# Keeping the output projection's weights in SBUF, and moving the sum of the keys

## The chip, the cores and the metric

The kernel runs on one core of one Trainium2 chip. The metric is the device time of one execution in microseconds (us); a number of executions is given as its median. All arithmetic is in float32.

## The reference

One decoder layer in three parts, each added to its input and followed by a layer norm. `x` is 4 sequences of 1024 tokens of width 512.

```python
# part 1: Mamba block with gated MLP
xz = rmsnorm(x) @ in_proj_w.T;  u, z = split(xz)          # 1024 channels each
u = silu(causal_conv(u, 4 taps) + conv_b)
dt_r, B, C = split(u @ x_proj_w.T);  dt = softplus(dt_r @ dt_proj_w.T + b)
h_t = exp(dt * A) * h_(t-1) + dt * B * u                  # 16 states per channel, over 1024 tokens
y = (sum over states of h * C + u * D) * silu(z)
h = x + y @ out_proj_w.T                                  # the output projection, 1024 -> 512
x = layernorm(x + h + (silu(n @ w1.T) * (n @ w2.T)) @ w3.T),  n = rmsnorm(h)
# part 2: cross attention on 64 keys, 16 heads; a temperature per head and sequence
scores = q @ k.T / sqrt(32)
feats = [mean of scores, mean of the row maxima, mean variance of softmax(scores)]
t = exp(clip(mlp(feats)));  attn = softmax(q @ k.T / (2 t))
x = layernorm(x + (attn @ v) @ Wo.T + bo)
# part 3: linear layer plus a mixture of 8 rank-16 experts, top 2
x = layernorm(x + x @ W.T + b + lora(x))
```

## The kernel before

The 4096 tokens are cut into 8 chunks of 512 (two to a sequence), and the work of each chunk into small units, each a few instructions on one or several engines. There are five streams of units, and every engine runs the units of all streams in one fixed order:

- the scan ("step", "sum", "gate"): 64 steps to a chunk, each for 2 blocks of 128 channels and one state. POOL (GpSimd) multiplies by B (L1194) and by C (L1204), ScalarE (ACT) makes the decays with an exponential (L1252), DVE (VectorE) runs the recurrence (L1558) and adds up the states (L1568). After 16 steps the gate (L1574) multiplies the finished pair of blocks by silu(z). Four gates make a chunk's y;
- the "f" stream: first the fronts of all 8 chunks (norm, transposes, "cv" and "z" blocks of the input projection with the convolution, the small projection "proj"), and only then, chunk by chunk, the output projection. Unit `("ou", c, half, q)` is piece q of 4 of its weights for half of chunk c's tokens: 4 matmuls at L1839. "out" adds x and squares (DVE L1585, ACT L1337), "rms" and "hs" make the norm (ACT L1344), "to" transposes (L1849);
- the "y" stream: the gated MLP ("h", "hv" at L1781, "w3" at L1878), its layer norm, "turn" (transposes, L1891) and the query projection (L1781);
- the "s" stream: scores for the statistics. For each of a chunk's 4 tiles of 128 tokens and each half of the heads: "sc1" (TensorE, L1914), "mx" (DVE maximum, L1640), "e1" (ACT exponentials, L1428), "sq" (DVE sum, L1653). "ent" closes the chunk. At every second chunk "mean" (L1668 to L1676) gathers the sequence's statistics into the tile `sta`, and "mlp" turns them into temperatures: 16 one-column matmuls at L1924, three small matmuls (L1929, L1931, L1933) with ScalarE between them, then "clip" and "temper" on DVE. The real scores "sc2" (L1914 too) of both chunks of the sequence wait for "temper". In the last chunk the half tiles go in a wider form: maximum (L1640), subtraction (L1643), ScalarE's exponential and square (L1415, L1418), two sums (L1651, L1653);
- the "x" and "w" streams: attention and experts of chunks 0 to 6 and of chunk 7.

"dt" units (L1828) prepare the scan's time steps.

The order is made before the kernel is built, by `schedule()`: a list scheduler with a cost for every part of a unit (`parts`), its needs, and a number for the place of each stream and chunk (`PHASE`, `WORK`, `LOOK`). It also gives out the four PSUM banks of the dense work. All DMAs are issued by SP, in one order (`loads()`), and an issue that waits holds those behind it. An engine waits only on semaphores of what it really reads, so a unit can start earlier or later than the scheduler thought, but never pass another on its engine.

What the change touches: the buffer `wmix` has two slots of 512 KB. Both the fronts (w_x and the blocks of in_proj_w) and the output projection take their weights through it (`f_weights`, `load_f` at L988), so the four pieces are loaded anew for each of 16 halves of a chunk, 64 loads of 512 KB, each waiting on a semaphore (`o_used`) until the slot's last user is done. `xnT` has two halves, used in turn by even and odd chunks: for the normalised input of the fronts, and later for the squares and the normalised sum in "out", "hs" and "to".

```python
wmix = sb("wmix", [P, FSLOTS, 1024])        # FSLOTS = 2
xnT = sb("xnT", [P, 2, KC, CH])
```

## Time and profile before

| what | us |
|---|---|
| median of 3 runs (lowest, highest) | 3610.53 (3606.46, 3612.91) |
| the profiled execution | 3614.06 |
| its span, from the first instruction to the last | 3612.0 |
| TensorE busy, matmuls | 3056.7 |
| DVE busy | 2799.0 |
| POOL busy | 2535.8 |
| ScalarE busy | 2137.4 |

The fronts fill the program up to about 819 us, with the scan of chunk 0 and most of chunk 1 beside them. From there to about 3165 us the scan of the other chunks runs beside the dense work of the chunks whose scan is done. The scan's last gate is followed by chunk 7's dense work alone, 447 us.

The matmuls are float32: every 128x512 matmul that the program has is executed as two in the trace, so 8 in a row of the trace are 4 of the program. The granted clock of TensorE is given as a share of full speed: 1.00 is 2.4 GHz, 0.50 the lower level, 1.2 GHz.

### The profile page before, as it was taken

What the parts mean: (1) busy time and instruction counts of PE and PEld (TensorE: products, weight loads), DVE (VectorE), ACT (ScalarE), POOL (GpSimd) and SP (SyncE); (2) the same over time, 40 slices, a digit from 0 to 9 for tenths busy, and PEclk for the clock granted to TensorE, in tenths of its full rate; (3) what the DMA queues carried; (4) which work ended last, traced back from release to release, by engine and by line L of the source; (5) the groups of instructions that cost most, each with busy time, mean ns of one, the idle gap of its engine ahead of it and who ended that gap; (6) DMA issues with size and microseconds to landing.
All of it is one profiled execution on the core that took longest, in us unless ns stands there. A gap on an engine that the chain in (4) does not pass through costs nothing.

```text
span 3612.0 us, 33154 instructions
## 1 busy us (share of the span) xinstructions
PE 3056.7 (85%) x8248; PEld 1460.9 (40%) x8248; DVE 2799.0 (77%) x3376; ACT 2137.4 (59%) x4824; POOL 2535.8 (70%) x1132
## 2 busy tenths in 40 slices
PE   6877677877988987899989868998994898999868
PEld 3433333333434433444434334444442444444444
DVE  3778888888898888888899888888898898822253
...
GB/s 174 145 171 201 188 187 199 186 188 221 221 186 147 174 210 132 129 164 147 195 154 184 204 111 146 166 149 177 160 190 110 162 159 162 168 76 76 41 1 24
DMA packets 247160, 558.49 MB, mean 155 GB/s; under 512 B 34748, under 2 KB 35132, under 8 KB 246716
## 3 DMA queue, kind: packets, MB, share of 16 engines
...
q14 instruction: 118, 0.97, 0.1%
...
## 4 chain that ended last, share of the span: by engine, by line
PE 38%; DVE 10%; ACT 9%; issue 4%; POOL 2%; DMA 0%; DVEq 0%; ACTq 0%; POOLq 0%; SPq 0%
PE ps L1781 22%; PE ps L1878 8%; DVE hb L1558 3%; PE ps L1839 3%; ACT ps L1428 2%; ACT xw L1467 2%; DVE ps L1568 1%; PE ps L1949 1%; PE ps L1914 1%; ACT ps L1252 1%; POOL hb L1194 1%; DVE mxs L1640 1%; PE ps L1982 1%; POOL hb L1204 1%; PE ps L1941 1%
## 5 line engine op out<-in xcount | busy, mean ns | idle before, releaser
L1204 POOL TENSOR_TENSOR hb<-hb,bc 128x1024 f32<-128x1024 f32 x512 | 1205.5, 2355 | 390.4 <-ACT state L1322 225.3
L1194 POOL TENSOR_TENSOR hb<-dtu,bc 128x1024 f32<-128x1024 f32 x512 | 1206.3, 2356 | 161.1 <-DVE ps L1568 153.2
L1781 PE MATMUL ps<-fT,wden 128*128 128x512 f32 x2304 | 1044.4, 608 | 78.9 <-DVE se L1653 25.7
L1252 ACT ACTIVATE ps<-dt,a_neg 128x512 f32<-128x512 f32 x1024 | 689.2, 690 | 588.0 <-DVE hb L1558 586.5
L1781 PEld LDWEIGHTS ps<-fT,wden 128*128 128x128 f32 x2304 | 442.6, 195 | 632.6 <-issue 611.1
L1558 DVE TENSOR_TENSOR_SCAN hb<-ps,state,hb 128x512 f32<-128x512 f32 x512 | 627.6, 1268 | 73.0 <-POOL hb L1194 38.8
L1558 DVE TENSOR_TENSOR_SCAN hb<-ps,hb 128x512 f32<-128x512 f32 x512 | 596.8, 1207 | 88.4 <-POOL hb L1194 63.8
L1568 DVE TENSOR_TENSOR ps<-ps,hb 128x1024 f32<-128x1024 f32 x512 | 624.6, 1220 | 11.6 <-POOL hb L1204 10.9
L1781 PE MATMUL ps<-xnT,wmix 128*128 128x512 f32 x1024 | 492.7, 642 | 81.6 <-DMA wmix<-in_w_mix 44.1
L1878 PE MATMUL ps<-wden,hm 128*128 128x512 f32 x1024 | 466.2, 608 | 34.2 <-DVE res L1611 14.8
L1781 PEld LDWEIGHTS ps<-xnT,wmix 128*128 128x128 f32 x1024 | 208.5, 207 | 361.9 <-issue 305.4
L1878 PEld LDWEIGHTS ps<-wden,hm 128*128 128x128 f32 x1024 | 194.6, 194 | 285.0 <-issue 229.3
L1839 PE MATMUL ps<-wmix,u 128*128 128x512 f32 x512 | 232.4, 604 | 6.6 <-DMA wmix<-in_w_mix 4.3
L1364 ACT ACTIVATE hm<-ps 128x512 f32<-128x512 f32 x128 | 76.0, 594 | 228.9 <-PE ps L1781 140.1
L1225 POOL TENSOR_TENSOR res<-res,bo_b 128x512 f32<-128x512 f32 x32 | 39.6, 1272 | 209.2 <-PE ps L1891 209.2
L1914 PE MATMUL ps<-kbd,qT 128*128 128x256 f32 x512 | 143.0, 418 | 41.9 <-DVE se L1653 28.9
L1611 DVE TENSOR_TENSOR res<-ps,res 128x512 f32<-128x512 f32 x128 | 87.5, 684 | 114.0 <-PE ps L1878 113.8
L1518 DVE SCALAR_TENSOR_TENSOR ps<-stage,cols,ps 128x512 f32<-128x512 f32 x192 | 144.5, 754 | 35.9 <-ACT ps L1284 31.2
L1467 ACT ACTIVATE xw<-ps,nm,ftv 128x64 f32<-128x64 f32 x384 | 149.1, 413 | 8.3 <-PE ps L1914 4.5
L1839 PEld LDWEIGHTS ps<-wmix,u 128*128 128x128 f32 x512 | 96.8, 193 | 131.9 <-issue 117.4
L1215 POOL TENSOR_TENSOR dtu<-dt,u 128x1024 f32<-128x1024 f32 x32 | 75.3, 2355 | 89.1 <-DVE dt L1546 89.1
L1914 PEld LDWEIGHTS ps<-kbd,qT 128*128 128x128 f32 x512 | 100.6, 207 | 78.9 <-DVE se L1653 34.6
...
## 6 DMA issues: line engine op xcount, KB each, us to landing
bc<-p_dram SPq DMA_DIRECT2D x1024, 256.0 KB, 3.4
...
wmix<-in_w_mix SPq DMA_DIRECT2D x128, 512.0 KB, 3.9
...
```

What stands on the lines that cost most here:

```text
L1194: TTn(hb[:, n % HB], dtu[:, :, :], bc[:, 0, n % BC].unsqueeze(1).broadcast_to([P, 2, CH]), ALU.mult).then_inc(s.s1_ready, 1)
L1204: TTn(hb[:, n % HB], hb[:, n % HB], bc[:, 1, n % BC].unsqueeze(1).broadcast_to([P, 2, CH]), ALU.mult).then_inc(s.s3_done, 1)
L1252: A_(dst, dt[:, p % 2, jj], ACT.Exp, scale=a_neg[:, j, n:n + 1]).then_inc(full_of(key), 1)
L1467: ins = A_(eb_of(c)[:, hh], bank[:, h], ACT.Exp, bias=nm2[:, TT * half + i, hh:hh + 1], scale=ftv[:, 0, hh:hh + 1], accum_out=den_of(c)[:, ...
L1518: ins = V.scalar_tensor_tensor(acc, up[:, i % 2, tap:tap + CH], conv_w[:, i, tap:tap + 1], acc, ALU.mult, ALU.add)
L1558: V.tensor_tensor_scan(hb[:, n % HB, jj], src, hb[:, n % HB, jj], first, ALU.mult, ALU.add).then_inc(free_of(key), 1)
L1568: V.tensor_tensor(ps[:, 2:4], ps[:, 2:4], hb[:, n % HB], ALU.add).then_inc(s.sum_done, 1)
L1611: V.tensor_tensor(res[:, c % 3, tt], src, res[:, c % 3, tt], ALU.add).then_inc(free_of(key), 1)
L1781: ins = M(dst, a, b, start=start and n == 0, stop=stop and n == len(pairs) - 1)
L1839: ins = M(ps[:, USE[key][0]], u[:, half, j, t * P:(t + 1) * P], wo[:, j % 2], start=j == 0, stop=j == JB - 1)
L1878: ins = M(dst, hm[:, f, tt * P:(tt + 1) * P], wi[:, (f % 2) * 512:(f % 2) * 512 + 512], start=f == 0, stop=f == FG - 1)
L1914: ins = M(dst[:, m * 256:(m + 1) * 256], qT[:, c4, T * P:(T + 1) * P], kbd[:, b % 2, c4], start=True, stop=True)
```

## The change

1. The four pieces of the output projection's weights are loaded once, after the last "z" block of the last chunk (`load_o`, one semaphore, waited for at 64 by the first output projection). Two lie in the two slots of `wmix`, two in the second half of `xnT`; both are free of the fronts by then. The 64 loads and their waits on `o_used` go.
2. Since the second half of `xnT` is taken, "out", "hs" and "to" of all chunks use its first half; the first square of chunk c waits for the last transpose of chunk c-1.
3. "mean" is split: a new unit "kmean" takes the sum of the keys, its product with the sum of the queries and the copies into `sta`. It stands behind the first tile's scores in the "s" stream. The two sums over maxima and entropies stay in "mean".
4. The numbers `WORK`, `PHASE` and `LOOK` are others, and the scheduler makes another order of the same units.

```diff
@@ s_plan
             for hf in range(2):
                 got += [("sc1", c, t, hf), ("mx", c, t, hf)] + [("e1", c, t, hf, q) for q in range(2 if wide1(c) else 3)]
                 got.append(("sq", c, t, hf))
+            if t == 0 and c % 2:
+                got.append(("kmean", c))
@@ parts
     elif kind == "ou":
-        part(PE, 4 * MM, ("gate", c, PAIRS - 1), ("res_load", c), ("f_load", F_FIRST.get(u)),
+        part(PE, 4 * MM, ("gate", c, PAIRS - 1), ("res_load", c), ("o_load", 0),
...
+    elif kind == "kmean":
+        part(DVE, 2.6, ("kv", b))
     elif kind == "mean":
-        part(DVE, 4.0, ("ent", c))
+        part(DVE, 1.0, ("ent", c))
@@ tables
-WORK = {"x": 849.2, "w": 145.7, "s": 1219.5, "y": 59.6, "f": 162.7}
+WORK = {"x": 531.5, "w": 166.1, "s": 1773.5, "y": 59.6, "f": 224.7}
...
-    "s": (36.876, 7.162, 16.712, 7.488, 1.167, 1.492, 6.161, -4.101),
+    "s": (35.117, 8.807, 16.82, 6.805, 0.505, 1.937, 6.955, -4.264),
@@ f_weights
-        elif kind == "ou":
-            first[u] = len(src)
-            src.append(W_O + u[3])
-            release.append((u, u))
@@ decoder_layer
+        w_o = [wmix[:, 0], wmix[:, 1]] + [xnT[:, 1, 2 * m:2 * m + 2].rearrange("p c l -> p (c l)") for m in range(2)]
@@ SP
+            def load_o():
+
+                filled(sp, ("z", CHUNKS - 1, JB - 1))
+                for q in range(PAIRS):
+                    sp.dma_start(w_o[q], A["w_mix"][W_O + q]).then_inc(s.wo_in, 16)
@@ ScalarE, "out" ("hs" and "to" likewise)
                     if i == 0:
-                        filled(act, ("z", CHUNKS - 1, JB - 1))
-                    A_(xnT[:, half, i], ht[:, i], ACT.Square, accum_out=smo[:, 0, i:i + 1]).then_inc(s.ss2_ready, 1)
+                        filled(act, ("ft", c - 1, KC - 1) if c else ("z", CHUNKS - 1, JB - 1))
+                    A_(xnT[:, 0, i], ht[:, i], ACT.Square, accum_out=smo[:, 0, i:i + 1]).then_inc(s.ss2_ready, 1)
@@ DVE
+                elif kind == "kmean":
                     dve.wait_ge(kv_in[b % 2], 64 * (b // 2 + 1))
...
                     V.tensor_reduce(ks[:, 0, :], kbd[:, b % 2, :, :], AX, ALU.add).then_inc(s.kb_sum, 1)
                     ch.link(V.tensor_tensor(ks[:, 1, :], qs[:, 0, :], qs[:, 1, :], ALU.add))
                     dve.wait_ge(s.kb_sum, b + 1)
                     ch.link(V.tensor_tensor(ks[:, 0, :], ks[:, 0, :], ks[:, 1, :], ALU.mult))
                     for q in range(4):
                         rows = slice(32 * q, 32 * q + 32)
-                        ins = V.tensor_copy(sta[rows, 0].rearrange("p (c q) -> p c q", q=4)[:, :, q], ks[rows, 0, :])
-                    ins.then_inc(s.sta_ready, 1)
+                        V.tensor_copy(sta[rows, 0].rearrange("p (c q) -> p c q", q=4)[:, :, q], ks[rows, 0, :])
+                elif kind == "mean":
+                    dve.wait_ge(s.ent_done, c + 1)
+                    dve.wait_ge(s.mx_ready, 2 * TT * (c + 1))
+                    V.tensor_reduce(sta[:, 1, :], mxs[:, :, :].rearrange("p t h -> p h t"), AX, ALU.add)
+                    V.tensor_reduce(sta[:, 2, :], ents[:, :, :].rearrange("p t h -> p h t"), AX, ALU.add).then_inc(s.sta_ready, 1)
@@ TensorE, "ou"
-                    wo = f_in(pe, F_FIRST[unit]).rearrange("p (j d) -> p j d", j=2)
+                    if c == 0 and i == 0 and q == 0:
+                        pe.wait_ge(s.wo_in, 16 * PAIRS)
+                    wo = w_o[q].rearrange("p (j d) -> p j d", j=2)
```

What the change moves is shown at three places. The line numbers of the new kernel are a few higher.

The first is SP's queue at the end of the fronts, around the last z blocks (z_dram<-ring stores them; bc<-p_dram are the scan's broadcasts of B and C). Before:

```order
L988 DMA wmix<-in_w_mix 128x1024
L1073 DMA bc<-p_dram 128x512
L1000 DMA z_dram<-ring 128x512 x2
L1065 DMA bc<-p_dram 128x512
L1073 DMA bc<-p_dram 128x512
L988 DMA wmix<-in_w_mix 128x1024
L1065 DMA bc<-p_dram 128x512
L1000 DMA z_dram<-ring 128x512 x2
L988 DMA wmix<-in_w_mix 128x1024
```

After:

```order
L1003 DMA z_dram<-ring 128x512 x2
L1068 DMA bc<-p_dram 128x512
L1076 DMA bc<-p_dram 128x512
L991 DMA wmix<-in_w_mix 128x1024 x2
L991 DMA xnT<-in_w_mix 128x1024 x2
L1068 DMA bc<-p_dram 128x512
L1003 DMA z_dram<-ring 128x512 x2
```

The three single loads shown before are pieces 0, 1 and 2 of the first projection; piece 0 is issued when the sixth z block is out. Now all four stand together where piece 1 stood, behind the wait for the eighth.

The second is TensorE in chunk 3's stage: from chunk 3's last transposes (ident,res), through chunk 4's projection (wmix,u), the scores of chunk 3 (kbd,qT x16 in all), chunk 4's transposes (ident,xnT) and hidden blocks (fT,wden, and of chunk 3 the query projection), to the statistics (ones_t,sta). Before, its second part:

```order
L1839 MATMUL ps<-wmix,u 128x512 x4
L1781 MATMUL ps<-fT,wden 128x512 x4
L1914 MATMUL ps<-kbd,qT 128x256 x16
L1849 MATMUL ps<-ident,xnT 128x128 x16
L1781 MATMUL ps<-fT,wden 128x512 x8
L1828 MATMUL ps<-proj,w_dt 128x512 x2
L1781 MATMUL ps<-fT,wden 128x512 x4
L1924 MATMUL ps<-ones_t,sta 3x1 x16
```

After:

```order
L1848 MATMUL ps<-xnT,u 128x512 x8
L1788 MATMUL ps<-fT,wden 128x512 x12
L1923 MATMUL ps<-kbd,qT 128x256 x2
L1858 MATMUL ps<-ident,xnT 128x128 x16
L1923 MATMUL ps<-kbd,qT 128x256 x6
L1788 MATMUL ps<-fT,wden 128x512 x12
L1923 MATMUL ps<-kbd,qT 128x256 x4
L1788 MATMUL ps<-fT,wden 128x512 x4
L1923 MATMUL ps<-kbd,qT 128x256 x4
L1788 MATMUL ps<-fT,wden 128x512 x20
L1933 MATMUL ps<-ones_t,sta 3x1 x16
```

The scores stood in one block ahead of the transposes; now transposes and hidden blocks stand between them, and the statistics come later.

The third is TensorE in chunk 5's stage, the same names one pair of chunks later (chunk 5's scores, chunk 6's projection). Before:

```order
L1914 MATMUL ps<-kbd,qT 128x256 x16
L1924 MATMUL ps<-ones_t,sta 3x1 x16
L1929 MATMUL ps<-tmp,t_w 64x16
L1839 MATMUL ps<-wmix,u 128x512 x4
L1828 MATMUL ps<-proj,w_dt 128x512
L1839 MATMUL ps<-wmix,u 128x512 x4
L1931 MATMUL ps<-tmp,t_w 128x16
```

After:

```order
L1923 MATMUL ps<-kbd,qT 128x256 x16
L1848 MATMUL ps<-wmix,u 128x512 x8
L1835 MATMUL ps<-proj,w_dt 128x512
L1848 MATMUL ps<-xnT,u 128x512 x8
L1835 MATMUL ps<-proj,w_dt 128x512
L1933 MATMUL ps<-ones_t,sta 3x1 x16
L1848 MATMUL ps<-wmix,u 128x512 x8
L1848 MATMUL ps<-xnT,u 128x512 x8
L1938 MATMUL ps<-tmp,t_w 64x16
L1940 MATMUL ps<-tmp,t_w 128x16
L1942 MATMUL ps<-tmp,t_w 128x16
L1858 MATMUL ps<-ident,xnT 128x128 x4
```

Half of the projection moved ahead of the statistics; the three small matmuls behind them moved together, right ahead of chunk 6's transposes.

## Rows read from the trace of the kernel before

**Rows 1.** The page, parts 1 and 5: engines, and the projection's group.

```profile
PE 3056.7 (85%) x8248; PEld 1460.9 (40%) x8248; DVE 2799.0 (77%) x3376; ACT 2137.4 (59%) x4824; POOL 2535.8 (70%) x1132
...
L1839 PE MATMUL ps<-wmix,u 128*128 128x512 f32 x512 | 232.4, 604 | 6.6 <-DMA wmix<-in_w_mix 4.3
```

**Rows 2.** Stretch, length; busy of PE, PEld, DVE, ACT, POOL; PEclk, DMA share, GB/s.

```profile
819.00:865.00 46.00, 32.12 (x71) 12.29 (x69) 37.85 (x40) 29.08 (x43) 44.62 (x22) 0.93 0.83 270
2067.00:2104.00 37.00, 17.08 (x46) 9.90 (x44) 31.16 (x35) 32.65 (x118) 35.34 (x17) 0.69 0.48 160
2104.00:2157.00 53.00, 41.04 (x121) 18.25 (x121) 43.06 (x57) 42.39 (x99) 34.85 (x16) 0.80 0.34 113
2746.00:2794.00 48.00, 12.04 (x34) 7.74 (x35) 45.84 (x55) 39.00 (x171) 46.36 (x21) 0.58 0.40 128
819.00:3165.00 2346.00, 2056.97 (x5636) 984.57 (x5635) 2013.97 (x2360) 1505.68 (x3583) 1995.72 (x884) 0.93 0.51 166
```

**Rows 3.** Timeline of TensorE, 819 to 870 us: start, us, group [idle before].

```profile
819.78 3.60 PE L1839 MATMUL ps<-wmix,u 128*128 128x512 f32 x8
824.23 18.39 PE L1839 MATMUL ps<-wmix,u 128*128 128x512 f32 x40 [0.85 <-DMA wmix<-in_w_mix]
...
844.25 3.70 PE L1839 MATMUL ps<-wmix,u 128*128 128x512 f32 x8 [0.57 <-DMA wmix<-in_w_mix]
...
850.17 3.70 PE L1839 MATMUL ps<-wmix,u 128*128 128x512 f32 x8 [1.17 <-DMA wmix<-in_w_mix]
868.99 1.33 PE L1849 MATMUL ps<-ident,xnT 128*128 128x128 f32 x5 [15.12 <-ACT xnT L1344]
```

**Rows 4.** SP's issue of piece 1, and DMA from 790 to 840 us.

```profile
819.98 0.33 SPq L988 DMA_DIRECT2D wmix<-in_w_mix  x1
...
GB/s 156 82 216 302 329 231 208 382 410 416 406 369 180 84 193 329 380 370 136 177 321 256 395 226 156 216 275 383 387 290 269 185 367 274 254 347 66 249 321 139
```

**Rows 5.** Timeline of TensorE in chunk 3's stage.

```profile
2083.71 2.08 PE L1914 MATMUL ps<-kbd,qT 128*128 128x256 f32 x4 [7.76 <-DVE se L1653]
2088.53 2.07 PE L1914 MATMUL ps<-kbd,qT 128*128 128x256 f32 x4 [2.75 <-DVE se L1653]
...
2103.09 1.09 PE L1849 MATMUL ps<-ident,xnT 128*128 128x128 f32 x4 [2.85 <-DVE se L1653]
```

**Rows 6.** Timeline of TensorE in chunk 5's stage.

```profile
2793.95 0.94 PE L1924 MATMUL ps<-ones_t,sta 128*3 128x1 f32 x32 [23.70 <-DVE sta L1676]
...
2795.66 6.36 PE L1839 MATMUL ps<-wmix,u 128*128 128x512 f32 x8
2801.95 1.12 PE L1828 MATMUL ps<-proj,w_dt 64*128 64x512 f32 x2
```

**Rows 7.** Timeline of DVE and of TensorE around chunk 7's statistics.

```profile
3422.22 0.68 DVE L1653 TENSOR_REDUCE se<-ps 128x8 f32<-128x512 f32 x1
3422.82 0.68 DVE L1640 TENSOR_REDUCE mxs<-ps 128x8 f32<-128x512 f32 x1
...
3425.53 0.69 DVE L1651 TENSOR_REDUCE se<-hm 128x8 f32<-128x512 f32 x1 [1.29 <-ACT ps L1418]
...
3452.31 1.21 DVE L1670 TENSOR_REDUCE ks<-kbd 128x4 f32<-128x1024 f32 x1
...
3453.82 0.69 DVE L1676 COPY sta<-ks 32x4 f32<-32x4 f32 x4
...
3454.65 0.94 PE L1924 MATMUL ps<-ones_t,sta 128*3 128x1 f32 x32 [29.75 <-DVE sta L1676]
...
3461.86 5.21 PE L1914 MATMUL ps<-kbd,qT 128*128 128x256 f32 x12 [2.67 <-DVE nm L1693]
```

**Rows 8.** Waits of POOL; the last gate (DVE); chunk 7's projection (TensorE).

```profile
POOL hb L1194 <- DMA bc<-p_dram: 5.1, 5, 3.0
...
3163.82 1.28 DVE L1574 SCALAR_TENSOR_TENSOR u<-ps,u 128x512 f32<-128x512 f32 x2
...
3165.48 7.03 PE L1839 MATMUL ps<-wmix,u 128*128 128x512 f32 x16
```

29 lines of the change are left out of this document (12 added, 17 removed), and 8 rows, old and new, of the table PHASE.

## Prediction

> **What bounds the kernel now.** I read the page first, then the idle time of TensorE by stage, then the timeline at the places the change touches. TensorE is the busiest engine, 3056.7 us of 3612.0 [rows 1]. In the middle of the program (819 to 3165 us) it is busy 2057.0 of 2346 us while DVE is busy 2014.0 and POOL 1995.7 [rows 2]: three engines at 85 to 88%, each with its own fixed queue, so that a wait on one is soon a wait on the others. TensorE's 289 us of idle time there are the only ones this change can turn into a shorter kernel. Three pieces of it stand out: 36.0 us between 2746 and 2794, where chunk 5's scores are followed by a wait of 23.70 us for its statistics [rows 2, 6]; 31.9 us (19.9 and 12.0) between 2067 and 2157, the same stage of chunk 3 [rows 2, 5]; and the end, where TensorE waits 29.75 us for chunk 7's statistics [rows 7]. The waits for the output projection's weights are small: 4.3 us in all before L1839 [rows 1].
>
> **The change, part by part.** All is summed against the profiled execution's own 3614.06 us (its span 3612.0 and 2.06 around it); the median of the runs is 3610.53, so the forecast is the median plus the sum.
>
> *The projection's loads.* 64 loads of 512 KB become four, all issued when the last z block is out of TensorE. Now that moment has one load, issued at 819.98 [rows 4], while TensorE already works on a piece fetched earlier (819.78); the next piece lets it go on at 824.23 [rows 3]. Afterwards the first projection waits for all four pieces (one semaphore at 64), and nothing stands between the last z block and that projection on TensorE. One piece took 4.25 us from issue to the matmul (824.23 less 819.98). Three more are 1.57 MB: at the highest rate seen in this stretch, 416 GB/s [rows 4], 3.8 us, so 8.0 us is the lower end; four in series, as if they shared nothing, are 17 us, the upper end. Stores and broadcasts for the scan are issued close behind and share the engines; I take 9.2 us, nearer to the lower end because that rate, held for several slices, shows that loads overlap. Against it stand the three waits of this projection that go: 0.85, 0.57 and 1.17 us [rows 3], 2.6 in all. After a pause TensorE starts at its lower clock: behind the 23.70 us wait eight matmuls took 6.36 us [rows 6] where eight at the full clock took 3.60 [rows 3]; for a pause of 9 us I take 1.4 of this 2.8 (bounds 0 and 2.8). Sum: +9.2 + 1.4 - 2.6 = **+8.0 us** (bounds +5.4 and +17.2). Nothing hides it: POOL is busy 44.6 of 46 us there [rows 2], and the chain from the projection through the norm to the transposes (15.12 us [rows 3]) simply starts later.
> The rule of the Trainium skill that speaks against this edit is in "DMA: Bandwidth & Descriptors", section "Rules for kernel authors": issue a transfer early and wait for it late. The kernel before does that for pieces 0 and 1; the new one can't, since their room is in use by the fronts. In the section "Anatomy of one DMA" of that page the Trainium skill fits a transfer, issued from GpSimd, as 2.0 us and its bytes at 436 GB/s; taking the four as one transfer that is an estimate of 6.8 us, and this term would be +5.6 instead of +8.0.
>
> *The other 60 loads.* They take with them the rest of the 4.3 us, 1.7 us: **-1.7**. Broadcasts of the scan wait behind fewer transfers; POOL waits for them 5.1 us in the whole program [rows 8], so I count nothing.
>
> *The sum of the keys.* At the end of chunk 7 its four kinds of instructions stand on TensorE's path: from 3452.31 to the end of the copies at 3454.51 they are 2.2 us [rows 7]. They move ahead of tile 1's maximum. But that is the same DVE queue in the same serial chain: half a tile is a maximum, a subtraction, a wait of 1.29 us for ScalarE and two sums, then the next maximum [rows 7], with no gap between the last sum of one and the maximum of the next, which is where the new unit stands. So the 2.2 us leave one link of the chain and enter another: **0** (bounds -1.3, if one ScalarE wait swallowed part, and +0.5). In chunks 1, 3 and 5 the scan's instructions are on this queue too; it is the same work at another place, and what it brings there is in the next two terms.
>
> *Chunk 5's stage.* Now TensorE stands at the statistics from 2770 to 2793.95. After, the first half of chunk 6's projection and two dt matmuls stand ahead of them: 16 matmuls in the program's order, which the trace executes as 32, at 0.45 us each (8 took 3.60 [rows 3]), are 14.4 us, and dt twice 1.12 [rows 6]. It also brings losses. The transposes of chunk 6 now follow its projection with only three small statistics matmuls between, and the norm ahead of them took 15.12 us where nothing covered it [rows 3]; I take half of that, 7.6. And these three statistics matmuls lose their filler: where nothing covers them, in chunk 7, 7.2 us pass from the first (3454.65) to the next scores (3461.86) [rows 7]; I take 4.8, since the first link stays covered. 14.4 + 2.2 + 2.8 (the cold start that goes) - 7.6 - 4.8 = 7.0: **-7** (bounds -19.4, the gains alone, and +2.9, the norm's 15.12 and the 7.2 in full against them).
>
> *Chunk 3's stage.* Now the score matmuls wait for each other's banks: 7.76 us once, 2.75 three times (one of them is shown), and 2.85 before the transposes [rows 5], 18.9 of the stage's 31.9 us of idle time [rows 2]. After, chunk 4's transposes and first hidden blocks stand between the scores, and the statistics come some five matmul groups later. The transposes then wait for their norm, with the query groups as cover; and the three statistics matmuls stand close together behind ScalarE. I take 10 of the 18.9 as gained, about half: **-10** (bounds -18.9, all of it, and +2.9 as in chunk 5).
>
> *The rest.* All other units of the tables keep their kinds and counts, in an order that differs in small swaps from chunk 0 to 6; from chunk 6's last transposes to the end TensorE's order is the same. **0**, bounds 8 either way. ScalarE's new wait (squares of chunk c behind the transposes of c-1) names something that is always long done.
>
> Sum: +8.0 - 1.7 + 0 - 7 - 10 + 0 = -10.7. 3610.53 - 10.7 = 3599.8, so **3600 us**.
>
> **The rivals.** *A, the gaps are the scan's.* TensorE's recovered gaps are worth something only if the scan comes forward too, since each chunk's projection waits for its last gate. If DVE and POOL set the pace behind 2067 us, TensorE waits a little later for the same gate and the -17 is given back, while the load at 819 us stays, in a stretch where POOL is full: 3610.5 + 8 - 1.7 = 3617, and 3618 with 1 us for the new links between the statistics matmuls; 3627 if the loads land in series. It decides from the point at which the last gate of chunk 6 follows the projection's third piece. For it: POOL's 44.6 of 46 us at the start, DVE busy 45.8 of the 48 us of chunk 5's stall [rows 2]. Against it: later, TensorE reaches chunk 7's projection at 3165.48, just behind the scan's last gate at 3163.82 [rows 8], and over the whole middle DVE is 86% and POOL 85% busy [rows 2], so both have room to follow.
> *B, half comes back.* Of the two stage terms only half is kept: 3610.5 + 8 - 1.7 - 8.5 = 3608. For it: the new order puts its own waits in (norm, statistics).
> *C, the delay at 819 is absorbed* by the pauses before chunk 0's and chunk 1's later transposes and both stages give near their outer ends: 3610.5 - 1.7 - 24 = 3585. Against it: those pauses are latency in series with the delay, not slack.
> *D, only the loads count*: the reordering is neutral and the load is as in A; that is A's time by another road and is counted there.
>
> **How the numbers follow.** A measurement of this kernel can tell about 0.2% (7.2 us) from no change. The forecast (3591 to 3603) has 0.45, C 0.12, B 0.24, A 0.19. Faster by over 0.2% (below 3603.3) is the forecast and C and a little of B's lower edge: 0.58; within 0.2%: 0.24; slower (above 3617.7): 0.18. The range reaches from C's inner side to A with a load at the middle of its bounds: 3580 to 3622.
>
> **What would show it.** Right: a pause of 8 to 11 us before the first L1848 matmul where now there is none, with four issues of L991 just ahead; the two statistics waits of TensorE down from 23.70 to a few us in chunk 5 and unchanged at 29 to 30 us in chunk 7, with the sum of keys inside tile 1 and the half tiles around it as long as now; TensorE's idle time from 2067 to 2157 of 32 us down to about 20; no wait for weights before any later projection. Wrong: the pause is 15 us or none; the tail from chunk 7's projection to the end is shorter than 447 us by over 1 us (then the keys did count); or the time of the last gate against the start has not moved while TensorE's gaps have (rival A).

## The result, and the profile after

The changed kernel takes **3637.66 us** (median of 5 runs, 3626.17 to 3642.05) where the kernel before takes 3609.62 beside it: a ratio of 1.0063, 95% interval 1.0048 to 1.0079. The medians are 28 us apart. The five runs of the changed kernel are few and spread over 16 us, and the ratio with its interval is a loss of 23 us, 17 to 29. The forecast of 3600 us and its range (up to 3622) were both wrong. The profiled execution has a span of 3635.9 us, against 3612.0 before.

The page's first line, busy times, DMA total and one group of its part 5 (against [rows 1]): the engines do the same work, and less is moved (527.02 MB against 558.49). TensorE is busy 7.6 us longer and idle 16.3 us longer. The group is w3; behind it, for comparison, the same group before: its waits grew from 34.2 to 54.2 us.

```profile
span 3635.9 us, 33028 instructions
...
PE 3064.3 (84%) x8248; PEld 1468.0 (40%) x8248; DVE 2792.5 (77%) x3376; ACT 2137.3 (59%) x4824; POOL 2535.2 (70%) x1132
...
DMA packets 238519, 527.02 MB, mean 145 GB/s; under 512 B 33788, under 2 KB 34172, under 8 KB 238076
...
L1887 PE MATMUL ps<-wden,hm 128*128 128x512 f32 x1024 | 475.9, 618 | 54.2 <-DVE dt L1551 27.7
```

```profile
L1878 PE MATMUL ps<-wden,hm 128*128 128x512 f32 x1024 | 466.2, 608 | 34.2 <-DVE res L1611 14.8
```

The same stretches as in [rows 2], shifted to where their work stands now (length; busy PE, PEld, DVE, ACT, POOL; clock, DMA share, GB/s). Chunk 3's stage (2087 to 2177) leaves TensorE idle for 6.6 and 14.5 us, 21.0 in place of 31.9. Chunk 5's (2765 to 2813) has 26.4 idle in place of 36.0. The stretches are of equal length but hold other instructions than before, so this tells how full they are and not how much was gained. And 819 to the last gate is 2369 us where it was 2346, and in it TensorE does 9 us more and idles 14 us more.

```profile
819.00:865.00 46.00, 32.13 (x68) 13.38 (x68) 32.11 (x32) 19.85 (x34) 39.60 (x19) 0.86 0.60 200
2087.00:2124.00 37.00, 30.43 (x90) 15.80 (x89) 28.65 (x36) 31.10 (x105) 26.64 (x12) 0.95 0.39 127
2124.00:2177.00 53.00, 38.54 (x112) 16.93 (x111) 46.03 (x54) 39.81 (x108) 40.63 (x19) 0.81 0.45 133
2765.00:2813.00 48.00, 21.61 (x46) 10.79 (x45) 44.67 (x51) 38.03 (x166) 43.06 (x20) 0.61 0.41 130
819.00:3188.00 2369.00, 2065.58 (x5641) 992.04 (x5642) 2006.82 (x2358) 1504.45 (x3582) 1993.96 (x883) 0.93 0.48 152
```

SP's issues and TensorE at the first projection (against [rows 3, 4]): the four pieces are issued from 818.69 to 820.45, and the first matmul starts at 827.05.

```profile
818.69 0.81 SPq L991 DMA_DIRECT2D wmix<-in_w_mix  x2
819.54 0.91 SPq L991 DMA_DIRECT2D xnT<-in_w_mix  x2
...
827.05 9.22 PE L1848 MATMUL ps<-wmix,u 128*128 128x512 f32 x16 [8.40 <-DMA xnT<-in_w_mix]
836.12 7.03 PE L1848 MATMUL ps<-xnT,u 128*128 128x512 f32 x16
...
874.71 1.54 PE L1858 MATMUL ps<-ident,xnT 128*128 128x128 f32 x6 [15.53 <-ACT xnT L1349]
```

TensorE in chunk 5's stage (against [rows 6]). The wait of 23.70 us for the statistics is gone, L1933 follows at once at 2820.93. What stands in its place is a row of others.

```profile
2771.58 2.07 PE L1923 MATMUL ps<-kbd,qT 128*128 128x256 f32 x4 [4.41 <-DVE se L1658]
...
2786.02 2.08 PE L1923 MATMUL ps<-kbd,qT 128*128 128x256 f32 x4 [7.54 <-DVE se L1658]
...
2801.86 9.97 PE L1848 MATMUL ps<-wmix,u 128*128 128x512 f32 x16 [8.94 <-issue]
...
2820.93 0.94 PE L1933 MATMUL ps<-ones_t,sta 128*3 128x1 f32 x32
...
2840.66 0.60 PE L1940 MATMUL ps<-tmp,t_w 64*128 64x16 f32 x2 [4.30 <-ACT tmp L1446]
2844.85 0.61 PE L1942 MATMUL ps<-tmp,t_w 64*128 64x16 f32 x2 [3.59 <-ACT tmp L1449]
2850.48 1.12 PE L1858 MATMUL ps<-ident,xnT 128*128 128x128 f32 x4 [5.02 <-ACT xnT L1349]
```

The last gate on DVE, and TensorE at chunk 7's statistics (against [rows 7, 8]): the gate ends 23.7 us later, and the wait behind it is as long as before.

```profile
3187.49 1.29 DVE L1579 SCALAR_TENSOR_TENSOR u<-ps,u 128x512 f32<-128x512 f32 x2
...
3478.82 0.94 PE L1933 MATMUL ps<-ones_t,sta 128*3 128x1 f32 x32 [29.62 <-DVE sta L1684]
```

**Where the time went, by stretch.** The marks are ends of instructions in each trace: the last z gate of chunk 7 (DVE L1579 of the kernel before), the start of the first output projection on TensorE, the last w3 sum (DVE L1611 of before) of chunks 0, 1, 3 and 5, the last gate of chunk 7, the end. The table has the lengths between them, in us; "before again" is a second trace of the kernel before, from a run below. Chunk 1's stage of scores and statistics lies in the column headed 3, chunk 3's in the column headed 5, and chunk 5's in "last gate".

| kernel | to first projection | to chunk 0's last w3 | chunk 1 | 3 | 5 | last gate | end |
|---|---|---|---|---|---|---|---|
| before | -1.5 | 257.5 | 255.7 | 678.0 | 700.2 | 453.9 | 446.9 |
| before again | -1.5 | 260.2 | 256.0 | 677.6 | 697.8 | 453.6 | 446.9 |
| **after** | 7.0 | 261.3 | 258.4 | 684.9 | 701.3 | 455.7 | 447.1 |
| e1: resident, old order | 7.3 | 256.0 | 255.7 | 678.0 | 693.5 | 460.5 | 450.0 |
| e7: the same, load early | -1.5 | 258.3 | 254.0 | 679.4 | 700.2 | 459.7 | 448.1 |
| e4: keys' sum, old order | -1.5 | 257.8 | 255.8 | 681.2 | 704.0 | 463.0 | 448.2 |
| e8: e4, one operand | -1.8 | 260.5 | 255.8 | 677.8 | 700.2 | 457.6 | 446.9 |
| e2: streamed, new order | -1.5 | 269.1 | 259.8 | 685.2 | 709.9 | 455.3 | 446.7 |
| e3: after, load early | -1.5 | 265.6 | 254.8 | 685.4 | 701.8 | 455.4 | 447.0 |
| e6: after, keys' sum back, load early | -1.5 | 265.7 | 254.8 | 684.2 | 706.6 | 451.6 | 447.2 |
| e5: after, keys' sum back | 7.7 | 260.3 | 258.2 | 691.6 | 701.9 | 451.6 | 447.2 |
| e11: after, one operand | 6.8 | 260.3 | 258.3 | 680.1 | 705.7 | 452.9 | 450.4 |
| e12: e11, load early | -1.5 | 263.8 | 258.2 | 680.1 | 702.4 | 452.8 | 450.4 |
| e13: after, chunk 1's projection held | 7.6 | 255.2 | 257.1 | 684.5 | 704.2 | 453.2 | 446.9 |
| e14: e13, load early | -1.5 | 258.7 | 256.8 | 684.3 | 701.8 | 455.4 | 447.0 |
| e16: e13, dt pairs held too | 7.2 | 255.2 | 257.1 | 683.2 | 706.6 | 455.3 | 447.1 |
| e17: e16, load early | -1.5 | 257.4 | 257.1 | 686.7 | 704.2 | 456.9 | 447.6 |
| e18: before, one half of xnT | -1.5 | 259.1 | 253.9 | 679.2 | 699.4 | 454.9 | 446.7 |
| e9: before, new numbers | -1.5 | 258.2 | 255.6 | 685.0 | 721.3 | 460.4 | 450.0 |
| e10: after, old numbers | 7.6 | 260.6 | 258.3 | 683.6 | 724.2 | 453.0 | 468.9 |

Against the mean of the two traces of before, the changed kernel loses 8.5 us at the first projection, then 2.4, 2.6, 7.1, 2.3 and 2.0, and 0.2 in the tail: 25.1, less 1.6 by which this execution reached the first mark early. So of the 28 us between the medians the two traces show 23.8.

### The profile page after: what moved, and what is told of

It reads as the page before. It is cut to its first block, busy times and chain, and to the rows that moved or that the text cites. A ratio compares the mean times of both kernels' runs of the same rounds, so it can differ in the third digit from the quotient of the medians.

```text
span 3635.9 us, 33028 instructions
## 1 busy us (share of the span) xinstructions
PE 3064.3 (84%) x8248; PEld 1468.0 (40%) x8248; DVE 2792.5 (77%) x3376; ACT 2137.3 (59%) x4824; POOL 2535.2 (70%) x1132
## 2 busy tenths in 40 slices
DMA packets 238519, 527.02 MB, mean 145 GB/s; under 512 B 33788, under 2 KB 34172, under 8 KB 238076
## 4 chain that ended last, share of the span: by engine, by line
PE 57%; DVE 16%; ACT 14%; issue 7%; POOL 3%; DMA 2%; SPq 0%; DVEq 0%; POOLq 0%; ACTq 0%
PE ps L1788 34%; PE ps L1887 10%; PE ps L1848 6%; DVE hb L1563 6%; DVE ps L1573 3%; DVE ps L1523 2%; POOL hb L1199 2%; ACT ps L1257 2%; ACT ps L1433 1%; ACT xw L1472 1%; PE ps L1923 1%; PE ps L1835 1%; POOL hb L1209 1%; PE ps L1958 1%; DMA wmix<-in_w_mix 1%
## 5 line engine op out<-in xcount | busy, mean ns | idle before, releaser
L1573 DVE TENSOR_TENSOR ps<-ps,hb 128x1024 f32<-128x1024 f32 x512 | 624.1, 1219 | 14.0 <-POOL hb L1209 13.4
L1887 PE MATMUL ps<-wden,hm 128*128 128x512 f32 x1024 | 475.9, 618 | 54.2 <-DVE dt L1551 27.7
L1887 PEld LDWEIGHTS ps<-wden,hm 128*128 128x128 f32 x1024 | 198.4, 198 | 316.2 <-issue 236.8
L1848 PE MATMUL ps<-wmix,u 128*128 128x512 f32 x256 | 121.9, 628 | 19.5 <-issue 9.8
L1835 PE MATMUL ps<-proj,w_dt 64*128 64x512 f32 x128 | 83.7, 738 | 60.9 <-DVE res L1538 14.6
## 6 DMA issues: line engine op xcount, KB each, us to landing
bc<-p_dram SPq DMA_DIRECT2D x1024, 256.0 KB, 3.4
z_dram<-ring SPq DMA_DIRECT2D x64, 256.0 KB, 4.5
```

The lines of the kernel that those rows point to most:

```text
L1573: V.tensor_tensor(ps[:, 2:4], ps[:, 2:4], hb[:, n % HB], ALU.add).then_inc(s.sum_done, 1)
L1835: M(dst, w_dt[0:64, i * P:(i + 1) * P], proj[0:64, half, :], start=True, stop=True).then_inc(full_of(key), 1)
L1848: ins = M(ps[:, USE[key][0]], u[:, half, j, t * P:(t + 1) * P], wo[:, j % 2], start=j == 0, stop=j == JB - 1)
L1887: ins = M(dst, hm[:, f, tt * P:(tt + 1) * P], wi[:, (f % 2) * 512:(f % 2) * 512 + 512], start=f == 0, stop=f == FG - 1)
```

## Experiments

All ratios are against runs of the kernel before on the same chip; e1 to e4 shared theirs (median 3608.19 us), e5 to e8 (3609.83), e9 to e12 (3610.31), e13 to e15 (3610.88), e16 and e17 (3607.82), and e18 (3611.85).

| run | median us | ratio | 95% interval |
|---|---|---|---|
| e1 resident, old order | 3620.21 | 1.0033 | 1.0022 to 1.0045 |
| e2 streamed, new order | 3643.64 | 1.0090 | 1.0060 to 1.0121 |
| e3 after, load early | 3626.08 | 1.0041 | 1.0026 to 1.0057 |
| e4 keys' sum, old order | 3623.76 | 1.0038 | 1.0027 to 1.0050 |
| e5 after, keys' sum back | 3640.95 | 1.0080 | 1.0060 to 1.0101 |
| e6 e5, load early | 3630.65 | 1.0051 | 1.0031 to 1.0070 |
| e7 e1, load early | 3616.93 | 1.0013 | 1.0001 to 1.0025 |
| e8 e4, one operand | 3617.18 | 1.0015 | 1.0002 to 1.0029 |
| e9 before, new numbers | 3651.60 | 1.0116 | 1.0101 to 1.0131 |
| e10 after, old numbers | 3676.76 | 1.0185 | 1.0170 to 1.0200 |
| e11 after, one operand | 3636.16 | 1.0073 | 1.0056 to 1.0089 |
| e12 e11, load early | 3630.04 | 1.0056 | 1.0041 to 1.0071 |
| e13 after, projection held | 3631.43 | 1.0049 | 1.0032 to 1.0066 |
| e14 e13, load early | 3623.76 | 1.0027 | 1.0011 to 1.0042 |
| e15 before again | 3610.89 | 0.9996 | 0.9979 to 1.0013 |
| e16 e13, dt pairs held too | 3631.87 | 1.0063 | 1.0042 to 1.0084 |
| e17 e16, load early | 3625.14 | 1.0042 | 1.0029 to 1.0056 |
| e18 before, one half of xnT | 3612.86 | 0.9996 | 0.9978 to 1.0014 |

**e15** comes first in reading, since it says what such a table can tell: the kernel before against itself. Its trace's marks lay up to 3.7 us from the first trace's.

> The kernel before, word for word. Its time is the kernel's own: a ratio of 0.999 to 1.001, so that 0.2 per cent is what a comparison of this kind can tell. Its trace against the one shown of before: if the first scans end 2 to 4 us earlier here as they did in the traces of every experiment, these few microseconds are the run's and not the edit's.

### The parts of the change one by one, in the old order

**e1: the weights resident, nothing else.** The planner still thinks of 64 loads, so the order is that of before; the program leaves them out and takes the pieces from the four places of the change.

```diff
 MIXER, BEGUN, DONE, ORDER, DENSE_TAKES = schedule()
+FRONTS = F_FIRST[("ou", 0, 0, 0)]
+F_SRC, F_RELEASE = F_SRC[:FRONTS], F_RELEASE[:FRONTS]
...
+    at(DONE[("z", CHUNKS - 1, JB - 1)], 1, "o_load", 0)
...
-                    wo = f_in(pe, F_FIRST[unit]).rearrange("p (j d) -> p j d", j=2)
+                    if c == 0 and i == 0 and q == 0:
+                        pe.wait_ge(s.wo_in, 16 * PAIRS)
+                    wo = w_o[q].rearrange("p (j d) -> p j d", j=2)
```

> The kernel before in its own order on every engine, with the one load of the four pieces and with xnT's first half for out, hs and to; nothing else of the change. Theory L (the pause at 819 us is the cause and passes through to the end): the pause costs about 7.3 us net at the first projection, later weight waits give 1.7 us back, so 3615 us, ratio about 1.0015, with the scan's gates 5 to 8 us late all the way. Theory O (the new order is the cause, and the pause is small or absorbed): 3608 to 3613, ratio 0.9995 to 1.001.

3620.21 us, 12 more than before and above both expectations. The pause is there (TensorE's first projection matmul in e1, from its timeline):

```profile
824.94 8.83 PE L1847 MATMUL ps<-wmix,u 128*128 128x512 f32 x16 [8.64 <-DMA xnT<-in_w_mix]
```

In the table it costs 8.8 us at the first mark. 2.9 of them come back at once, and 5.5 in the stretch to chunk 5 (693.5 against 700.2 and 697.8); then 6.7 and 3.1 are lost in the last two.

**e4: the sum of the keys, nothing else.** Its place alone is moved, to where the change has it.

```diff
+for c_ in range(1, CHUNKS, 2):
+    ORDER[DVE].insert(ORDER[DVE].index(("sq", c_, 0, 1)) + 1, ("kmean", c_))
```

> The kernel before with the sum of keys alone moved behind the first tile's second half, all else in its old order. My prediction: no change, 3608 to 3612, since the 2.2 us only change their link in the chain of chunk 7 and cost other DVE time in chunks 1, 3 and 5. Rival (it shortens the statistics' chain): 2 to 9 us faster.

3623.76 us, 16 more, where I had counted nothing. The tail is hardly the place (448.2 for 446.9); the stages of chunks 1, 3 and 5 are, with 3.4, 5.0 and 9.2 us. (This trace is of the slowest of its ten runs, 3631.12.) Timeline of DVE, then of POOL, in chunk 1 of e4:

```profile
1388.33 1.21 DVE L1670 TENSOR_REDUCE ks<-kbd 128x4 f32<-128x1024 f32 x1
1389.45 1.62 DVE L1671 TENSOR_TENSOR ks<-qs 128x4 f32<-128x4 f32 x1
1391.11 0.16 DVE L1673 TENSOR_TENSOR ks<-ks 128x4 f32<-128x4 f32 x1
1391.30 0.69 DVE L1676 COPY sta<-ks 32x4 f32<-32x4 f32 x4
...
1388.70 2.35 POOL L1196 TENSOR_TENSOR hb<-dtu,bc 128x1024 f32<-128x1024 f32 x1
```

The sum of four columns (L1671) takes 1.62 us, until POOL's multiplication ends at 1391.05. In chunk 3 it takes 1.90 us, from 2092.54 to 2094.44, and POOL's row ends at 2094.42. In the kernel before, the same instruction takes 0.15 us in chunks 1, 3 and 7 and 0.47 in chunk 5, at a place where POOL mostly stands still, and the four kinds together take 2.2 to 2.5 us. Here they take 3.67, 3.94 and 4.75 in chunks 1, 3 and 5, and 2.2 in chunk 7, where the scan is over.

**e8: the same place, with one operand.** Is the wait for POOL the cost?

```diff
-ch.link(V.tensor_tensor(ks[:, 1, :], qs[:, 0, :], qs[:, 1, :], ALU.add))
+ch.link(V.tensor_reduce(ks[:, 1, :], qs[:, :, :].rearrange("p h c -> p c h"), AX, ALU.add))
...
-ch.link(V.tensor_tensor(ks[:, 0, :], ks[:, 0, :], ks[:, 1, :], ALU.mult))
+for q in range(KC):
+    ins = V.tensor_scalar(ks[:, 0, q:q + 1], ks[:, 0, q:q + 1], ks[:, 1, q:q + 1], None, ALU.mult)
+ch.link(ins)
```

> The kernel before with the keys' work alone moved behind the second half tile's sum (as in the run that cost 15 us), but the 128x4 sum of qs as a reduce of one operand and the 128x4 product as four tensor_scalar of one column each, so that no instruction of it reads two SBUF tensors. In the run with two operands the 128x4 sum took 1.62, 1.90 and 2.70 us in chunks 1, 3 and 5 instead of 0.15, each time until a GpSimd multiply of 2.35 us ended. Theory G (VectorE waits there for GpSimd when an instruction reads two SBUF tensors, and this is passed on): the rows stay under 0.2 us, the block at 2.2 to 2.6 us instead of 3.7 to 4.8, and of the 15.6 us at least 5.7 come back: 3612 to 3618 us. Rival W (it is the place in the score chain that costs, a small wait more or less is absorbed): rows short, time 3621 to 3625 us.

DVE and POOL in chunk 3 of e8:

```profile
2092.75 0.15 DVE L1671 TENSOR_REDUCE ks<-qs 128x4 f32<-128x8 f32 x1
2092.94 0.58 DVE L1674 TENSOR_SCALAR ks<-ks 128x1 f32<-128x1 f32 x4
2093.55 1.64 DVE L1678 COPY sta<-ks 32x4 f32<-32x4 f32 x4
...
2092.29 2.35 POOL L1196 TENSOR_TENSOR hb<-dtu,bc 128x1024 f32<-128x1024 f32 x1
```

The reduce and the column products do not wait for POOL, but now the first of the four copies does: they take 1.64 us instead of 0.69, and the first ends with POOL's row. So the wait moved, and the blocks are 3.30, 3.57 and 4.37 us, only 0.37 to 0.38 shorter each. The time is 3617.18 us, 6.6 us better than e4, in the range that theory G gave, but not by its means: 1.1 us of direct gain do not make 6.6, and the two intervals overlap a little. The three stages lose 0, 1.2 and 3.8 us here where e4's lost 3.4, 5.0 and 9.2. What a small shift of this block sets off behind it is open. That DVE waits for POOL here is shown; that this wait is the 16 us is not.

### The order

**e2: the new order with the 64 loads.** The changed planner, with the streamed loads put back in the program.

```diff
+for u_ in f_plan():
+    if u_[0] == "ou":
+        F_FIRST[u_] = len(F_SRC)
+        F_SRC.append(W_O + u_[3])
+        F_RELEASE.append((u_, u_))
```

> The changed kernel with its new order on every engine and its moved sum of keys, but the projection's weights streamed through wmix in 64 loads as before. Theory L: without the pause at 819 us most of the loss goes, 3612 to 3618. Theory O: the loss stays, less the 7 us of the pause, and the weight waits of the earlier and denser projections come on top (before the change: 4.3 us in another order): 3625 to 3635.

3643.64 us, above both expectations: the loss is there without any pause. It is no clean proof, since in this order TensorE waits 20.4 us, in 11 places, for the streamed weights at L1856, where the kernel before waits 4.3. That the pause is not the main cause rests on e3, e6 and e7 below.

**e3: the changed kernel with piece 0 early.** Piece 0 goes into its slot two z blocks sooner, and each piece has a semaphore of its own.

```diff
-    at(DONE[("z", CHUNKS - 1, JB - 1)], 1, "o_load", 0)
+    at(DONE[("z", CHUNKS - 1, JB - 3)], 1, "o_load", 0)
+    at(DONE[("z", CHUNKS - 1, JB - 1)], 1, "o_load", 1)
...
-                        pe.wait_ge(s.wo_in, 16 * PAIRS)
+                        pe.wait_ge(wo_in[q], 16)
```

> The changed kernel with one edit: piece 0 is loaded two z blocks earlier, into the slot of wmix that is free by then, and each piece has a semaphore of its own, so that the first projection starts with piece 0. The pause of 8.4 us at 819 us should be under 2 us. Theory L: the whole gain of 6 to 8 us arrives at the end, ratio about 1.004 where the change has 1.006. Rival: the engines are so coupled later that an earlier start is given back, ratio 1.006 again.

3626.08 us: 11.6 of the 28 us by the medians. The intervals of the ratios overlap, and of the 12.2 us between the two traces 4.8 lie ahead of the first mark; behind it the early load brings 7.4.

**e7: the same early load in the old order.**

> The kernel before with the four weight pieces resident, in the old order, piece 0 loaded two z blocks earlier. Against the resident kernel in the old order without it (3620.2 us). Theory P (its loss is the pause before the first output projection, passed on one to one): 3609 to 3613 us, first output projection at most 1 us late. Rival (the loss is in the lost second half of xnT, or the later SP order): the pause goes, the end stays at 3617 to 3621 us.

3616.93 us, 3.3 better than e1 (the intervals overlap) and 7 worse than before. Theory P falls and the rival holds, to within 0.1 us: the pause is gone (-1.5 at the first mark), but in the old order all but about half a microsecond of it had been given back by chunk 5's last w3, and the 6 us of the stretch to the last gate stay (459.7).

**e5 and e6: the changed kernel with the keys' sum back at the end of the statistics,** without and with the early load. `kmean` keeps its place in the order and does nothing there; `mean` is that of before.

> The changed kernel with the sum of the keys put back at the end of the chunk's statistics (its place in the program's order stays, but it does nothing there); residency, tables and the planner's order are the change's. Theory K (the keys' work in front of the second score tile costs 15 us in either order): 3637.7 - 15 = 3622 us, and no DVE row of 1.6 to 2.7 us for the 128x4 sum of qs. Theory O (the new order is what costs, the keys cost only in the old one): 3633 us or more.

> The same, and piece 0 of the output projection's weights loaded two z blocks earlier, each piece with a semaphore of its own. If both costs simply add (theory K, and 11.6 us for the early load as in the run before): 3622 - 11.6 = 3610.5 us, as the kernel before. If the new order is worth anything by itself, below 3608. Theory O: 3622 or more.

3640.95 and 3630.65 us: theory K falls, theory O holds. In the new order, taking the keys' sum out of the scores gains nothing (3637.66 with it). e1 and e4 add up to +28 as the change does, and this agreement is a coincidence: e6 has neither the pause nor the keys' place, and is still 14 us above e7, which has the same program in the old order. That is the price of the new order with the early load, and there the intervals are clear of each other; without it, e5 against e1, it is 21 us.

**e11 and e12: the one-operand form in the changed kernel,** without and with the early load.

> The changed kernel, with the 128x4 sum and product of the keys' work written with one SBUF operand each, as in the run in the old order that gave 6.6 us back. The rows of 1.63, 1.91 and 2.72 us should go to under 0.2. If each microsecond of the chain is passed on as there: 3637.7 - 6 = 3631 us. If the keys cost nothing in the new order (putting them back gained nothing there): 3636 to 3640 us.

> The run before with piece 0 of the weights two z blocks earlier and a semaphore for each piece, the change as well mended as the findings so far allow without a new order. 3626.1 us without the one-operand form; with it 3620 us if that is passed on, 3625 if not. Not below 3610 by any theory, since the new order's loss stays.

3636.16 and 3630.04 us (3637.66 and 3626.08 without the form): nothing, as e5 had it. In both traces the stretch to chunk 3's last w3 is 4.8 and 5.3 us shorter than without the form (680.1), and it is lost again behind it (705.7 in e11, a tail of 450.4 in both).

**e9 and e10: rules and numbers apart.** The order comes out of the rules (`parts`: what a unit needs) and the numbers (`WORK`, the five rows of `PHASE`, `LOOK`). e9 gives the kernel before the change's numbers; e10 gives the changed kernel those of before.

```diff
-WORK = {"x": 849.2, "w": 145.7, "s": 1219.5, "y": 59.6, "f": 162.7}
+WORK = {"x": 531.5, "w": 166.1, "s": 1773.5, "y": 59.6, "f": 224.7}
...
-LOOK = {"m": 0.319, "l": 0.0, "x": 0.0, "w": 0.043, "s": 0.009, "y": 0.096, "f": 0.0}
+LOOK = {"m": 0.313, "l": 0.0, "x": 0.0, "w": 0.049, "s": 0.058, "y": 0.123, "f": 0.023}
```

> The kernel before (streamed pieces, keys at the end of the statistics) with the change's numbers for the planner alone: its work sums, its five rows of offsets and its look-ahead. TensorE's order has 141 of 1208 steps moved, the first behind turn 0 (residency's own steps move 146, the first before it). Theory T (the numbers suit the changed kernel only and cost here): 3616 to 3622 us, later from chunk 2 on. Rival R (numbers are neutral, the 19 us that the new order cost with the keys back come from the steps that residency sets free, such as ou 1 wholly ahead of h 0 6): 3606 to 3613 us.

> The changed kernel with the numbers of before for the planner (work sums, offsets, look-ahead); residency and the keys' early place stay, and TensorE's order keeps ou 1 wholly ahead of h 0 6. Theory T (the new numbers cost): 3620 to 3628 us. Rival R (the steps set free cost, the new numbers are neutral or mend a part): 3637 us or more.

| | numbers of before | numbers of the change |
|---|---|---|
| before (streamed, old rules) | 3610 | 3652 |
| changed (resident, new rules, keys' sum moved) | 3677 | 3638 |

e9 went the way of theory T and e10 the way of rival R, which were meant to exclude each other, and both by much more than expected. Each set of numbers suits its own rules: with the old numbers the changed program would cost 66 us, the new ones bring 39 of them back, and the same new numbers cost the kernel before 41. In both off-diagonal cases the stretch from chunk 3 to chunk 5 has the largest loss (721.3 and 724.2 against 699); e10 loses 22 more in the tail. It can't be said from these runs which number does it.

**e13 and e14: one place put back.** With residency, the rules no longer tie chunk 1's output projection to its loads, and the planner puts all of it ahead of TensorE's `h 0 6`; before, it stood among `h 0 7` to `h 0 8`. The edit ties it there again. Only 8 of TensorE's 1208 steps, 19 of DVE's and 9 of ScalarE's differ from the changed kernel.

```diff
         part(PE, 4 * MM, ("gate", c, PAIRS - 1), ("res_load", c), ("o_load", 0),
-             takes=
+             *((("h", 0, 7 + i),) if c == 1 else ()), takes=
```

> The changed kernel, in which the planner may place chunk 1's output projection only behind h 0 7 (first half) and h 0 8 (second half), as it stood before; outside this piece the order of all engines is the change's. Theory E (the early projection starves the VectorE work of dt and hidden blocks, and this is passed on): no wait of 4.7 us before w3 near 1034, turn 0 at most 7 us later than before instead of 11.1, and the end 4 to 8 us earlier: 3630 to 3634 us. Rival G (given back by turn 1, since the projection is only done earlier): turn 0 earlier, turn 1 and the end as in the changed kernel, 3636 to 3639 us.

> The same with piece 0 of the weights loaded two z blocks earlier and a semaphore for each piece; against the run without the hold (3626.1 us). Theory E: 3618 to 3622 us, turn 0 at most 1 us later than in the kernel before. Rival G: 3624 to 3628 us.

TensorE around 1030 us, in the changed kernel and then in e13. The two dt rows (L1835) stood directly ahead of w3 (L1887), which waited 4.71 us for DVE to read their bank; with 8 matmul rows between, the wait is gone.

```profile
1028.09 1.12 PE L1835 MATMUL ps<-proj,w_dt 64*128 64x512 f32 x2
1033.92 6.47 PE L1887 MATMUL ps<-wden,hm 128*128 128x512 f32 x8 [4.71 <-DVE dt L1551]
```

```profile
1026.82 1.12 PE L1835 MATMUL ps<-proj,w_dt 64*128 64x512 f32 x2
1027.87 3.70 PE L1788 MATMUL ps<-fT,wden 128*128 128x512 f32 x8
1031.70 3.70 PE L1887 MATMUL ps<-wden,hm 128*128 128x512 f32 x8
```

e13 is 3631.43 us: 6.2 less, and in the trace 6.1 less (255.2 against 261.3) between the first projection and chunk 0's last w3, carried to the end. Theory E holds by the trace; by the times the intervals of e13 and of the changed kernel overlap. With the early load (e14, 3623.76, against 3626.08 for e3) only 2.3 us are left, between the two expectations, and in the traces the next stretch gives 2.0 of 6.9 back.

**e16 and e17: two more such places.** In chunk 3 the dt pairs of chunks 4 and 5 stand one step nearer to a w3 than before the change, with waits of 3.57 and 4.71 us there. The edit ties them back.

```diff
-        part(PE, FG * MM, ("hm", c, FG * i + FG - 1),
+        part(PE, FG * MM, *((("dt", 4, 5 + u[3]),) if u[:3] == ("w3", 3, 0) and u[3] in (1, 2) else ()), ("hm", c, FG * i + FG - 1),
...
-        part(PE, 4 * MM, ("to", c, KC - 1), ("load", ("h", *key)), takes=(bank,))
+        part(PE, 4 * MM, ("to", c, KC - 1), ("load", ("h", *key)), *((("dt", 5, int(kind == "hv")),) if key == (3, 12) else ()), takes=(bank,))
```

> As the run that held chunk 1's projection (3631.4 us), and in chunk 3's hidden blocks the dt pairs of chunks 4 and 5 stand one step earlier among w3 3 0 and h 3 12, as before the change. Theory D (a dt directly ahead of a w3 makes TensorE wait for VectorE, and this is passed on): the waits of 3.6 us near 1888 and 4.7 us near 1973 go to about 1 to 2.4 us, turn 3 at 2031 to 2033 instead of 2036, the end 2 to 6 us earlier, 3625 to 3629 us. Rival S (the scan sets turn 3 and the waits only show it): waits gone or moved, turn 3 and the end unchanged, 3630 to 3633 us.

> The same with piece 0 of the weights two z blocks earlier and a semaphore for each piece; against 3623.8 us (held projection, early load). Theory D: 3618 to 3621 us. Rival S: 3622 to 3626 us. Not below the kernel before by either.

3631.87 and 3625.14 us against 3631.43 and 3623.76: nothing. TensorE in e16:

```profile
1869.51 2.07 PE L1835 MATMUL ps<-proj,w_dt 64*128 64x512 f32 x2 [3.40 <-ACT ps L1332]
...
1883.38 6.55 PE L1887 MATMUL ps<-wden,hm 128*128 128x512 f32 x8 [4.16 <-DVE dt L1551]
```

The second wait (near 1979) went, the first stayed at 4.16 with a new one of 3.40 ahead of it, and the stretch shortened by 1.3 us (683.2), given back by chunk 5. The time is as rival S has it. Its reading, that the waits there only showed that the scan was late, fits, but with one of the two waits still in place e16 does not prove it.

**e18: the single half of xnT alone,** in the kernel before.

```diff
-                        filled(act, ("z", CHUNKS - 1, JB - 1))
+                        filled(act, ("ft", c - 1, KC - 1) if c else ("z", CHUNKS - 1, JB - 1))
-                    A_(xnT[:, half, i], ht[:, i], ACT.Square, accum_out=smo[:, 0, i:i + 1]).then_inc(s.ss2_ready, 1)
+                    A_(xnT[:, 0, i], ht[:, i], ACT.Square, accum_out=smo[:, 0, i:i + 1]).then_inc(s.ss2_ready, 1)
```

> The kernel before, streamed and in its old order, in which the norm behind the output projection uses half 0 of xnT alone, with ScalarE's new wait for the transposes of the chunk before, as residency needs it. Theory X (the single half costs in chunk 6): the stretch from chunk 5's last w3 sum to chunk 7's last gate takes 459 to 461 us instead of 453.9, and the time is 3614 to 3618 us. Rival Q (it is the missing loads, through SyncE's queue and what they shift): 453 to 455 us there and 3608 to 3612 us.

3612.86 us, and 454.9 us in the stretch in question: the single half costs nothing. By elimination the 6 us that e1 and e7 lose there come with the missing loads (rival Q), alone or together with the single half; by what road is open.

No kernel was faster than the one before. The best with the weights resident is e7, at 1.0013.

## Why the prediction was wrong

**The load's pause: right in size.** Forecast +8.0 in the first projection. Measured: a pause of 8.40 us (I took 9.2) and a cold start, 16 matmuls in 9.22 us where 16 at the full clock take 7.03. From the first projection matmul to the transposes is 47.7 us where it was 49.2, since the three waits went. 8.5 less 1.5 is +7.0. The trace has 8.4 us from the first issue to the matmul, inside my bounds from rows (8.0 to 17). The fit in the Trainium skill ("DMA: Bandwidth & Descriptors", section "Anatomy of one DMA"), which is for a transfer issued from GpSimd, would have been an estimate of 6.8. The rule in its section "Rules for kernel authors", issue early and wait late, is borne out: following it gave 11.6, 10.3, 6.1, 7.7 and 6.7 us in the new order (e3, e6, e12, e14, e17, each against its twin) and 3.3 in the old one (e7).

**The other 60 loads: right in the waits, wrong in the sum.** The 8.40 is all that L1848 waits for DMA, so the 1.7 us of waits did go. But residency without the pause is not 1.7 us cheaper than the kernel before, it is 7 us dearer (e7, interval 0.4 to 9), 6 of them in the stretch to the last gate. The forecast had no term for that, and its cause is open (e18).

**The sum of the keys: right in the tail, the step that failed is the sentence on chunks 1, 3 and 5.** The tail is 447.1 against 446.9 us, the wait 29.62 against 29.75. "The same work at another place" is wrong: with POOL busy beside it the block takes 3.67, 3.96 and 4.77 us in the changed kernel instead of 2.2 to 2.5. In chunk 5 of the changed kernel:

```profile
2777.39 2.72 DVE L1674 TENSOR_TENSOR ks<-qs 128x4 f32<-128x4 f32 x1
...
2777.76 2.33 POOL L1209 TENSOR_TENSOR hb<-hb,bc 128x1024 f32<-128x1024 f32 x1
```

In the old order the move alone costs 16 us (e4). In the new one it costs nothing that e5 and e11 could show.

**Chunk 3's and chunk 5's stages: the gaps closed as forecast, and nothing came of it. The step that failed is the one that turned TensorE's idle time into time of the kernel.** Chunk 3's idle time went from 31.9 to 21.0 us ("down to about 20"), chunk 5's from 36.0 to 26.4, its 23.70 us wait vanished. I counted -17. By the table, the stretches in which they lie became 2.3 and 2.0 us longer.

The sign that I had named for rival A, gaps closed and the last gate not earlier, is what came, and I gave A 0.19. But its mechanism, the scan setting the pace, is not shown. In the stretch to the last gate DVE is idle 74 us in the changed kernel and 63 before, POOL 90 and 77. What the traces do show is waits that the new order puts in, which is rival B's ground; all of the gain is gone, though, where B kept half. In the stretch with chunk 3's stage, TensorE waits 9.7 us for DVE's sums of the scores (L1658) where it was 24.7; its waits for DVE to read a dt bank (L1551) went from 5.1 to 27.2. 17.1 us of these stand at one place, where the last two dt units of chunk 5 follow each other with nothing between and a w3 follows them. Before, a hidden block of chunk 4 (`h 4 8`) and a product of chunk 2's attention stood between and behind them, which the new order has ahead of both. The changed kernel, then the same two units before:

```profile
2253.33 2.04 PE L1835 MATMUL ps<-proj,w_dt 64*128 64x512 f32 x2 [8.60 <-DVE dt L1551]
2263.87 5.90 PE L1887 MATMUL ps<-wden,hm 128*128 128x512 f32 x8 [8.50 <-DVE dt L1551]
```

```profile
2221.40 1.12 PE L1828 MATMUL ps<-proj,w_dt 64*128 64x512 f32 x2
2222.45 3.70 PE L1781 MATMUL ps<-fT,wden 128*128 128x512 f32 x8
2226.08 1.12 PE L1828 MATMUL ps<-proj,w_dt 64*128 64x512 f32 x2
2227.13 3.70 PE L1781 MATMUL ps<-watt,xw 128*128 128x512 f32 x8
```

No run puts this place back, so what it costs is not shown; e13 and e16 say that such a wait can be worth its length or nothing. In chunk 5's stage the new waits are of other kinds. The 8.94 us ahead of chunk 6's projection end with a sum of the scores (L1658 on DVE, done at 2801.76, the matmul starts at 2801.86); 4.30 and 3.59 are the links between the small statistics matmuls, 7.9 us where I had taken 4.8, and 5.02 is the norm, where I had taken 7.6. The statistics were ready 55.7 us after the first score matmul, where it was 47.7. Against the kernel before, this stage's stretch lost 2.0 us. Against the resident kernel in the old order (e1 and e7, 460.5 and 459.7) it is 4 to 5 us shorter in the changed kernel and 8 to 9 in e5 and e6 (451.6). So the -7 may well have been earned there and spent on the 6 us that residency costs in the same stretch; for chunk 3's stage no such gain shows (701.3 against 693.5 and 700.2).

**The rest of the order: 0 was wrong, and so were its bounds of 8.** The stretches that I put down as small swaps lost 2.4, 2.6 and 7.1 us. The runs give 14 us for the new order as a whole (e6 against e7; 21 without the early load), chunk 3's and chunk 5's stages included. 6 us of it, or 2 with the early load, come from one place that the difference of the orders shows plainly: a projection of 16 matmuls moved as a block, so that two dt matmuls came to stand directly ahead of a w3 (e13, e14). Where the 7.1 us between chunk 1 and chunk 3 come from is open: TensorE's waits for DVE's reading of dt grew by 7.3 us there, from 13.4 to 20.7, but the two places that e16 put back gave nothing.

One path through the runs adds up: residency with the early load in the old order +7 (e7), the new order +14 (e6), the late load +10 (e5), the keys' sum -3 (the changed kernel, within the noise) make 28. So 6 to 12 us are the load, the one term that was right. The largest part is the order that the change brought: it was set to -17 for two stages and to zero for the rest, on the ground that swaps are small. Rival A's own time (3617 to 3627) was over 10 us short, since it had no price for the order either.
